# Wider products of zeros ahead of the first gate, and three of W2's four loads issued later on ScalarE's queue

## The reference, cut to what matters

```
gate = relu(cond @ W3 + b3)                       # 64 x 512
v    = (64 * x + x.sum(axis=1)) * gate[:, None]   # 64 x 64 x 512
x1   = relu(v @ W2 + b2)                          # W2: 512 x 512
y1   = x1 @ w_up.T + b_up + (x1 @ A_up) @ B_up    # 2048 columns, w_up from 4-bit codes and scales
x2   = relu(y1)
y2   = x2 @ w_down.T + b_down + (x2 @ A_down) @ B_down
out  = x + y2
```

## Time and profile before

| | |
|---|---|
| median of 3 runs | 748.3 us (747.27 to 748.65) |
| the profiled execution | 747.43 us |
| its span, first to last instruction | 745.5 us |
| TensorE, busy | 739.8 us (99%), 3274 products |
| VectorE, busy | 554.3 us (74%) |
| ScalarE, busy | 419.7 us (56%) |
| GpSimd, busy | 77.5 us (10%) |

### The profile page before, as it was taken

How to read it: one execution, slowest core, us unless ns; L and a number is a source line. 1 busy time by engine, 2 the same in 40 slices (tenths; PEclk the granted TensorE clock), 3 DMA queues, 4 the chain that set the end, 5 groups by cost and what they waited for, 6 DMA issues and landing times. The chain is left out here.

```text
span 745.5 us, 9634 instructions
## 1 busy us (share of the span) xinstructions
PE 739.8 (99%) x3274; PEld 612.8 (82%) x3274; DVE 554.3 (74%) x727; ACT 419.7 (56%) x727; POOL 77.5 (10%) x69
## 2 busy tenths in 40 slices
PE   9999999999999999999999999999999999999998
PEld 8888878878888888888888888888888888888886
DVE  6997866778948488677867697867775877757596
ACT  5963384766562565758556275666646353535540
POOL 0065533243420000000000000000000000000000
PEclk9999999999999999999999999999999999999999
DMA  9969979888464997655407896666516697555663
GB/s 293 323 177 341 337 231 285 260 254 277 157 208 144 376 340 223 215 190 191 158 29 255 291 377 221 224 198 197 184 58 195 223 382 226 190 191 191 194 196 128
DMA packets 92242, 170.21 MB, mean 228 GB/s; under 512 B 8418, under 2 KB 25186, under 8 KB 91682
## 3 DMA queue, kind: packets, MB, share of 16 engines
q1 hardware_dynamic: 91330, 168.20, 68.2%
q10 hardware_dynamic: 864, 1.39, 0.6%
HBM read 129.71 MB, written 40.89 MB: 229 GB/s over the span
## 5 line engine op out<-in xcount | busy, mean ns | idle before, releaser
L1187 PE MATMUL ps<-x_hi,ring 128*128 128x512 f32 x672 | 261.7, 389 | 0.2
L1188 PE MATMUL ps<-x_lo,ring 128*128 128x512 f32 x672 | 261.5, 389 | 0.0
L1189 PE MATMUL ps<-x_hi,ring 128*128 128x512 f32 x672 | 261.4, 389 | 0.0
L1187 PEld LDWEIGHTS ps<-x_hi,ring 128*128 128x128 f32 x672 | 126.1, 188 | 27.4 <-ACT ps L527 1.0
L1189 PEld LDWEIGHTS ps<-x_hi,ring 128*128 128x128 f32 x672 | 126.1, 188 | 26.2
L1188 PEld LDWEIGHTS ps<-x_lo,ring 128*128 128x128 f32 x672 | 126.1, 188 | 26.0
L410 ACT ACTIVATE xt<-xt,gated,gate_n 128x64 f32<-128x64 f32 x216 | 74.6, 431 | 34.8 <-DVE gated L781 34.8
L519 ACT ACTIVATE f<-ps,small_in 128x512 f32<-128x512 f32 x96 | 64.8, 691 | 41.7 <-PE ps L1189 41.7
L972 DVE TENSOR_TENSOR x_lo<-x_sum,x_hi 128x512 fp32r<-128x512 f32 (+1 forms) x96 | 76.7, 818 | 4.2 <-ACT x_hi L557 3.4
L893 DVE TENSOR_TENSOR ps<-s,ps 128x512 f32<-128x512 f32 x48 | 33.3, 693 | 49.6 <-PE ps L1189 49.3
L930 DVE TENSOR_TENSOR res<-ps,res 128x512 f32<-128x512 f32 x71 | 47.6, 687 | 20.1 <-PE ps L1189 19.8
(11 more groups left out here) (90 smaller groups left out, 1020.5 us busy)
## 6 DMA issues: line engine op xcount, KB each, us to landing
ring<-made_w SPq DMA_DIRECT2D x336, 256.0 KB, 3.8
made_w<-made SPq DMA_DIRECT2D x16, 1280.0 KB, 6.0
xt<-in_x SPq DMA_DIRECT2D x32, 256.0 KB, 6.2
code<-in_codes SPq DMA_DIRECT2D x16, 512.0 KB, 8.5
scale<-made_s SPq DMA_DIRECT2D x16, 512.0 KB, 8.1
made_w<-plain SPq DMA_DIRECT2D x64, 128.0 KB, 6.3
res<-in_x SPq DMA_DIRECT2D x4, 2048.0 KB, 10.2
out<-res SPq DMA_DIRECT2D x12, 512.0 KB, 5.4
```

The costliest lines, as they stand in the source:

```text
L1187: pe.matmul(dest, w_hi, a_hi, start=start, stop=False, skip_group_check=True)
L1188: pe.matmul(dest, w_hi, a_lo, start=False, stop=False, skip_group_check=True)
L1189: return pe.matmul(dest, w_lo, a_hi, start=False, stop=stop, skip_group_check=True)
```

## The change

The tile `warm` becomes float32r of 128 x 640 (before: float32, 128 x 192), and each product of zeros takes 512 columns in place of 64. There are 7 and 3 of them in place of 8 and 5. Of W2's four loads the first stays where it was on ScalarE's queue. The second is issued behind `gate_tile(0)`, the third behind `x_high(0, 0)`, the fourth behind `w2_high(1)`.

```diff
-        warm = sb("warm", [P, 3 * SEQ], F32, "f")
+        warm = sb("warm", [P, P + T], F32R, "f")
...
-            for k in range(KD):
+
+            def load_raw_w2(k):
                 act.dma_start(raw_w2[:, k, :], w2[:, k, :]).then_inc(w2_raw[k], 16)
+
+            load_raw_w2(0)
             act.wait_ge(small_loaded, 16)
...
             gate_tile(0)
+            load_raw_w2(1)
             w2_high(0)
             x_high(0, 0)
+            load_raw_w2(2)
             for k in range(1, KD):
                 gate_tile(k)
             act.wait_ge(gate_done, KD)
             act.mul(gate_n[:], gate[:], float(SEQ)).then_inc(gate_done, 1)
             w2_high(1)
+            load_raw_w2(3)
             x_modulate(0, 1)
...
-            pool.memset(warm[:], 0.0).then_inc(zeroed, 1)
+            pool.memset(warm[:].bitcast(F32), 0.0).then_inc(zeroed, 1)
...
-                    mm = pe.matmul(ps[3][:, 0:SEQ], warm[:, 0:P], warm[:, P:P + SEQ], start=True, stop=True)
+                    mm = pe.matmul(ps[3][:], warm[:, 0:P], warm[:, P:P + T], start=True, stop=True)
                 mm.then_inc(warmed, 1)

             pe.wait_ge(zeroed, 1)
-            zeros(8)
+            zeros(7)
             pe.wait_ge(small_loaded, 16)
             for m in range(KD):
                 if m == 1:
-                    zeros(5)
+                    zeros(3)
                     pe.wait_ge(w3_loaded, 16)
```

## The result

The changed kernel takes 753.0 us (median of 5 runs, 752.78 to 753.47), the kernel before 748.3 (5 runs, 747.27 to 749.68): a ratio of 1.0065, 95% interval 1.0054 to 1.0077, so 4.9 us slower by the ratio (4.7 between the medians). 747.2 was forecast. Its profiled span is 751.0 us, 5.5 more than before.

What follows compares the result with a forecast made beforehand. TensorE was taken as busy throughout, its start bound by a chain from zeros through gate to W2's second tile. Gains of 0.75 (low clock) to 1.4 us (high), middle 1.1, gave 746.3, plus 0.9 for the median: 747.2 us; range 746.0 to 748.9.

Steps and rivals of the forecast that it cites:

- W2's loads on the queue: ScalarE's queue: W2's second load, issued at about 5.75 us, lands 3.8 us later at 9.55; later issues cost 0.1 us.
- W2's second tile lands late: ScalarE's cast of W2's second tile waits for its load: 748.7 us, or 751.6 at an 8.6 us landing time; chance 0.08.
- the clock falls again: TensorE idles some 2.5 us before W2's second tile; slow products behind cost 2.0 us: 748.9 us; chance 0.2.
- The zeros' part: TensorE's start: zeroing 0.4 us later, fewer wide zeros, gate earlier; 0.75 us won at the low clock, 1.4 at the high.
- Does it carry through: Behind the start: VectorE's row to 35.13 us and later transfers move along by the same amount, so the gain stays whole.

Runs made afterwards that it cites:

- the filled gap: The changed kernel with 28 more wide products of zeros between W2's first and second tile of products: 750.84 us, ratio 1.0041 against the kernel before.

## Why the prediction was wrong

**The step that failed** is "W2's loads on the queue": a landing of 3.8 us after issue was taken, "a load alone on ScalarE's queue does not stand behind SyncE's row of loads". It took 7.6. The step rested on two rows. One was a load issued when both queues were empty; the other was even sharing between queues whose loads had been issued side by side. Neither shows a load issued on a nearly empty queue after a row of loads on the other one. That case has two parts: 3 us and more without a packet, then half of a rate that two loads of its own queue divide. The bounds were right to reach to 8.6 us, and the choice between them was wrong: the nearest row in kind was a load with others ahead of it, because others were ahead of it, if on the other queue.

**The rival "W2's second tile lands late"** is what happened. Its point of decision (a landing past 11.1 us) and its price (by its way of counting 2.6 us for a landing at 13.6, measured 2.59 in the trace) held; its chance of 0.08 was far too small.

**The rival "the clock falls again"** happened on top. It was priced as part of a case in which the load is on time, at 2.0 us; it cost 2.3 in the trace and 1.8 to 2.2 by the filled gap. Its point of decision, a gap of about 2.2 us, did not hold: gaps of 1.94 and 1.95 us were enough, and one of 3.08 was not in the profiled execution. The two rivals were held to be alternatives, but the first makes the second: a longer wait for a load is a longer gap. The sum of both, 748.3 + 2.6 + 2.0 = 752.9, was not among the cases; 753.0 was measured.

**The zeros' part was right.** The zeroing took 0.63 us, TensorE began at 1.41, the first zeros were 0.43 us apart, the last gate tile started at about 8.1. What they bring was put at 0.75 to 1.4 us; the zeros alone brought 0.8 to 1.2 us (by the ratio and between the medians), though the interval reaches to nothing. That the forecast of 1.1 lies there is partly luck: it was taken as the middle between two levels of the clock.

**"Does it carry through"** held for the loss (5.0 us at 40 us, 5.5 at the end). For the gain it was taken too simply: from 1.5 to 0.55 us between 21 and 111 us in one pair of profiles.

**The rule of the Trainium skill** (TensorE: Matmul & The Clock Gate, Part 1) that the warm-up is a matter of time and not of a number of matmuls: narrow zeros left the pace low here too, 0.21 us up to 9.59. But the wide ones did not always raise it (by the gate's last products in six profiles of seven), and narrow 7 and 3 were as fast as wide 7 and 3. For the time of this kernel the rule's answer, that width brings nothing, stands; for the clock the trace still speaks against it.

## What to carry to other kernels

A load that is moved behind other work has to be priced by what all queues have issued ahead of its new place, not by what is ahead of it on its own queue; the loads that the next step waits for are the last ones to delay. A wait that grows in front of TensorE is to be priced with the clock behind it, as one case and not as two. And when the first part of a chain is made faster, look at what its next member waits for: here the gate came 2 us early and met a load that came 5 us after it was wanted.

## What the runs showed of the hardware that was not expected

- A load of 256 KB issued on ScalarE's queue at 6.01 us, with SyncE's queue full, moved no packet from 6.5 to 9.5 us and landed 7.6 us after issue (6.9 with the loads alone moved; 8.0 with only the second late, behind two of its own queue; 7.6 for the third where the second was early). With SyncE's issues from the scales on held, it moved none from 6.5 to 8 us and landed after 4.1.
- The same row of wide zeros had raised the clock by the gate's last products in six profiles (0.105 us apart in the changed kernel's) and not in the seventh (0.20 apart).
- Idle gaps of TensorE of 1.94, 1.95, 3.46 and 6.78 us each came with a stretch at a granted clock of 0.50; gaps of 1.30 and 3.08 us did not in the profiled executions, though others of the same two kernels have mean clocks of 0.995 to 0.998. The length of the gap alone doesn't tell whether the clock falls. What does was not tried.
- Products of zeros, whose results nobody reads, hold the clock as real ones do: with 28 of them in the long gap and 8 in the short one the granted clock read 1.00 where it had been 0.50.
